# One kernel, three layers on one core: three small GpSimd operations taken off, the bulk work on the routed output put elsewhere in GpSimd's order, and a second buffer for y

## The reference, cut to what matters

```python
def layer1(x):                                   # x: (16, 512, 128)
    z = _rmsnorm(x_normed, gamma1) @ W_in.T
    gate, xc = z[..., :256], z[..., 256:]
    xc = causal_conv4(xc) + conv_b
    alpha = exp(-8 * softplus(forget_base) * sigmoid(forget)); beta = sqrt(1 - alpha**2 + 1e-6)
    h = linear_recurrence(alpha, beta * sigmoid(inp) * xc)      # a scan over tokens
    x_h = x_normed + (gelu(gate) * h) @ W_out.T
    t   = x_h + (gelu(mgate) * mx) @ W_shrink.T                  # of rmsnorm(x_h) @ W_grow.T
    x3  = x + layernorm(t)
    y   = router_weight * (layernorm(x3) @ w_expert + b_expert)  # top-1 of 8, capacity 100 of all tokens
    return x3 + layernorm(y)
```

## Time and profile before

| | us |
|---|---|
| median of 3 runs (1336.96 to 1337.99) | 1337.04 |
| the profiled execution, its own time | 1337.33 |
| its span, first to last instruction | 1335.6 |
| granted TensorE clock, mean | 0.975 |
| busy in the span: PE / DVE / ACT / POOL | 1182.7 / 1096.2 / 976.9 / 824.4 |
| layer 1's iterations 1 to 15 and the drain | from about 900 to the end |

### The profile page before, as it was taken

How to read it: one execution, slowest core, us unless ns; L and a number is a source line. 1 busy time by engine, 2 the same in 40 slices (tenths; PEclk the granted TensorE clock), 3 DMA queues, 4 the chain that set the end, 5 groups by cost and what they waited for, 6 DMA issues and landing times.

```text
span 1335.6 us, 25924 instructions
## 1 busy us (share of the span) xinstructions
PE 1182.7 (89%) x8560; PEld 481.8 (36%) x8560; DVE 1096.2 (82%) x2355; ACT 976.9 (73%) x1780; POOL 824.4 (62%) x1091
## 2 busy tenths in 40 slices
PE   1689999999999999999999998997989999999962
PEld 0223232333333333333333332333544555555542
DVE  3877999999999999999999999965676867867757
ACT  1267887787788878788778878778767778787750
POOL 6304447466466566565665655276688898998863
PEclk9889999999999999999999999899999999999986
DMA  1131011011010110110110110000000000000000
GB/s 50 52 90 43 28 44 41 30 43 40 29 44 32 37 43 33 38 45 30 41 45 27 37 35 16 2 1 1 1 0 17 8 11 15 9 16 9 9 17 24
DMA packets 52516, 37.86 MB, mean 28 GB/s; under 512 B 8864, under 2 KB 51744, under 8 KB 52384
## 3 DMA queue, kind: packets, MB, share of 16 engines
q1 hardware_dynamic: 52384, 36.22, 8.5%
HBM read 6.31 MB, written 4.19 MB: 8 GB/s over the span
## 4 chain that ended last, share of the span: by engine, by line
PE 35%; POOL 20%; DVE 20%; issue 13%; ACT 8%; SPq 4%; DMA 0%; ACTq 0%; POOLq 0%; DVEq 0%
PE bank_pair L201 10%; PE bank L182 9%; DVE neg_max L493 9%; PE bank_pair L169 4%; PE bank_pair L228 3%; SPq L644 3%; PE bank_pair L210 3%; POOL probs L1574 3%; ACT probs L381 2%; PE bank_pair L235 2%; POOL rs_y L1546 2%; DVE probs L1181 1%; DVE y_q L472 1%; PE bank_pair L800 1%; POOL x_all L1523 1%
## 5 line engine op out<-in xcount | busy, mean ns | idle before, releaser
L381 ACT ACTIVATE probs<-bank 128x512 f32<-128x512 f32 x1024 | 569.3, 598 | 165.8 <-PE bank L182 163.3
L493 DVE TENSOR_REDUCE neg_max<-bank_pair 128x2 f32<-128x1024 f32 x512 | 610.6, 1216 | 87.3 <-PE bank_pair L169 85.4
L182 PE MATMUL bank<-q_stack,k_stack 50*128 50x512 bf16 x1024 | 352.7, 388 | 30.3 <-ACT probs L381 22.6
L201 PE MATMUL bank_pair<-probs,v_pad 128*32 128x256 f32 x4096 | 332.0, 394 | 0.4 <-issue 0.4
L169 PE MATMUL bank_pair<-k_stack,q_stack 48*128 48x512 bf16 x1024 | 291.4, 395 | 35.0 <-DMA k_stack<-k_parts 17.9
L182 PEld LDWEIGHTS bank<-q_stack,k_stack 50*128 50x128 bf16 x1024 | 79.4, 93 | 273.9 <-ACT probs L381 232.6
L201 PEld LDWEIGHTS bank_pair<-probs,v_pad 128*32 128x32 f32 x4096 | 82.9, 108 | 167.6 <-issue 161.1
L800 PE MATMUL bank_pair<-probs,w_gates 128*128 128x512 f32 x256 | 116.8, 600 | 2.0 <-issue 1.7
L567 POOL TENSOR_SCALAR tiny<-mv_b 128x4 f32<-128x4 f32 x16 | 3.7, 230 | 147.4 <-DVE mv_b L52 147.4
L522 POOL TENSOR_TENSOR q_rest<-q_rest,q_parts 128x512 f32<-128x512 f32 x16 | 20.2, 1265 | 118.6 <-ACT q_rest L325 118.6
L169 PEld LDWEIGHTS bank_pair<-k_stack,q_stack 48*128 48x128 bf16 x1024 | 53.8, 94 | 60.2 <-DVE neg_max L493 38.3
(11 more groups left out here) (253 smaller groups left out, 2217.3 us busy)
## 6 DMA issues: line engine op xcount, KB each, us to landing
q_stack<-q_parts SPq DMA_DIRECT2D x384, 32.0 KB
k_stack<-k_parts SPq DMA_DIRECT2D x384, 32.0 KB
x_all<-in_z_dram SPq DMA_DIRECT2D x16, 256.0 KB, 3.0
out_dram<-x_all SPq DMA_DIRECT2D x16, 256.0 KB, 2.3
q_stack<-max_rows SPq DMA_DIRECT2D x64, 8.0 KB
w_gates<-in_w_gates_dram SPq DMA_DIRECT2D x1, 512.0 KB, 3.5
w_in<-in_w_in_dram SPq DMA_DIRECT2D x1, 256.0 KB, 2.6
w_grow<-in_w_grow_dram SPq DMA_DIRECT2D x1, 256.0 KB, 3.9
```

Source lines behind the costliest of these rows:

```text
L182: nc.tensor.matmul(st_ps[h][:, :], k_stack[par][rows, p, c * P:(c + 1) * P], q_stack[par][rows, p, :], start=True, stop=True).then_inc(s[" ...
L201: mm = nc.tensor.matmul(acc[32 * g:32 * g + 32, cols], v_pad[bpar][:, kc, 4 * a + g, :], probs[:, at + g, cols], start=(t == 0 and kc == 0 ...
L381: nc.scalar.activation(probs[:, 4 * (n % RING) + g, :], st_ps[g % 2][:, :], ACT.Exp, scale=SCALE)\
L493: nc.vector.tensor_reduce(neg_max[j // 4][:, c, j % 4, :], score_ps[c % 2][:, :, :], AX_X, ALU.max, negate=True).then_inc(s["max_read"], 1)
```

## The change

On GpSimd three 128x4 operations of an iteration go: the scaling in `norm_h` (ScalarE's squares now carry the scale, so that their sum is the mean) and the two additions of epsilon in `rsqrt`, which VectorE does instead as `var_eps`, directly behind the statistics of t and of x3. y now alternates between two buffers by the iteration's parity (the second in q_stack), and its statistics too; VectorE waits for the subtraction of two batches ago instead of the last. With that the subtraction of the mean and the 128x512 product of batch i-4 leave the place ahead of `gate_mul(i)`. They run in iteration i+1: the first, `routed_mean`, behind `x_normed`, the second, `routed_product`, behind `root_t`. `x4_late` goes from behind `x_normed` to behind `x3_sum`, `root_ahead` from ahead of `x3_sum` to behind `root_x3`. The drain gets an order of its own.

```diff
@@ names
+    y_odd = ahead[:, T:2 * T]
@@ scalar(): mean_square
-                    A(xn2[:, c * D:(c + 1) * D], zx[par][:, c * D:(c + 1) * D], ACT.Square, accum_out=h_sum[:, c:c + 1])\
+                    A(xn2[:, c * D:(c + 1) * D], zx[par][:, c * D:(c + 1) * D], ACT.Square, scale=D ** -0.5,
+                      accum_out=h_sum[:, c:c + 1])\
@@ vector()
+        def var_eps(name, b):
+            wait(dve, s[f"stat_{name}"], C * (b + 1))
+            TS(rs[name][:, 0, :], stats[name][1][:, :, 1], EPS, None, ALU.add).then_inc(s[f"rs_{name}_step"], 1)
@@ y_of
-            return (acc_y, "y_odd") if i == NB + 2 else (y, "y")
+            return (y, y_odd)[i % 2], ("y", "y_odd")[i % 2]
@@ stats_y
+                wait(dve, s["rs_y_step"], 5 * (i - 4) - 8)
@@ routed (VectorE)
-                if i > NB + 1:
+                if i > NB + 2:
                     wait(dve, s["x4_ready"], b - 1)
                 else:
-                    wait(dve, s["yc_ready"], b)
+                    wait(dve, s["yc_ready"], b - 1)
@@ stats_t, and stats_x3 likewise
+                var_eps("t", i - 3)
@@ exps_inv
-                wait(dve, s["rs_y_step"], 5 * b)
+                wait(dve, s["rs_y_step"], 5 * b - 4)
@@ pool(): rsqrt
-            TS(r[:, 0, :], mv[:, :, 1], EPS, None, ALU.add).then_inc(q, 1)
@@ norm_h
-                TS(r[:, 0, :], h_sum[:, :], 1.0 / D, None, ALU.mult).then_inc(q, 1)
-                TT(r[:, 2, :], r[:, 0, :], half_neg, ALU.pow).then_inc(q, 1)
+                TT(r[:, 2, :], h_sum[:, :], half_neg, ALU.pow).then_inc(q, 2)
@@ routed_root, routed_sum
-                if i > NB:
-                    return
-                wait_apart(gp, s["x4_ready"], b, past_wait)
-                TT(rows(acc_y), rows(y), per_token(stats["y"][1][:, :, 0]), ALU.subtract).then_inc(s["yc_ready"], 1)
+        def routed_mean(i):
+            if live(i, -4):
+                b = i - 4
+                wait_apart(gp, s["stat_y"], C * (b + 1), past_wait)
+                wait_apart(gp, s["x4_ready"], b, past_wait)
+                TT(rows(acc_y), rows((y, y_odd)[i % 2]), per_token(stats[("y", "y_odd")[i % 2]][1][:, :, 0]), ALU.subtract).then_inc(s["yc_ready"], 1)
-        def routed_sum(i):
+        def routed_weight(i):
...
                 TT(rs["y"][:, 2, :], rs["y"][:, 1, :], top[:, 7, :], ALU.mult).then_inc(s["rs_y_step"], 1)
+        def routed_product(i):
...
                 TT(rows(acc_y), rows(acc_y), per_token(rs["y"][:, 2, :]), ALU.mult).then_inc(s["yn_ready"], 1)
                 if i >= NB:
                     x4(b)
@@ order of an iteration on GpSimd
             x_normed(i)
-            x4_late(i)
+            routed_mean(i - 1)
             norm_h(i)
             root_t(i)
+            routed_product(i - 1)
+            x3_sum(i)
+            x4_late(i)
+            root_x3(i)
             root_ahead(i)
-            x3_sum(i)
-            root_x3(i)
             roots_ahead(i)
             routed_root(i)
-            routed_sum(i)
+            routed_weight(i)
             gate_mul(i)
```

More of the change, by code:

```diff
@@ L1326, in stats_x3 @@
                 aggregate("x3", "x3", i - 3)
+                var_eps("x3", i - 3)
         def gated_in(i):
@@ L1478, in rsqrt @@
         def rsqrt(name, b):
-            q, mv, r = s[f"rs_{name}_step"], stats[name][1], rs[name]
-            wait_apart(gp, s[f"stat_{name}"], C * (b + 1), past_wait)
-            TS(r[:, 0, :], mv[:, :, 1], EPS, None, ALU.add).then_inc(q, 1)
+            q, r = s[f"rs_{name}_step"], rs[name]
             wait_apart(gp, q, 2 * b + 1, past_wait)
@@ L1503, in norm_h @@
                 wait_apart(gp, s["stat_h"], C * (b + 1), past_wait)
-                TS(r[:, 0, :], h_sum[:, :], 1.0 / D, None, ALU.mult).then_inc(q, 1)
-                wait_apart(gp, q, 2 * b + 1, past_wait)
-                TT(r[:, 2, :], r[:, 0, :], half_neg, ALU.pow).then_inc(q, 1)
+                TT(r[:, 2, :], h_sum[:, :], half_neg, ALU.pow).then_inc(q, 2)
                 wait_apart(gp, q, 2 * b + 2, past_wait)
@@ L1540, in routed_root @@
                 wait_apart(gp, s["stat_y"], C * (b + 1), past_wait)
-                var = stats["y_odd" if i == NB + 2 else "y"][1][:, :, 1]
+                var = stats[("y", "y_odd")[i % 2]][1][:, :, 1]
                 TT(top[:, 5, :], top[:, 4, :], var, ALU.mult).then_inc(q, 1)
@@ L1576, in pool @@
         if drain:
+            routed_mean(NB - 1)
+            routed_product(NB - 1)
             x4_late(NB)
-            routed_root(NB)
-            routed_sum(NB)
             norm_h(NB)
             gate_mul(NB)
+            routed_root(NB)
+            routed_weight(NB)
             root_t(NB)
+            routed_mean(NB)
             x3_sum(NB)
+            routed_product(NB)
             norm_h(NB + 1)
@@ L1592, in pool @@
             routed_root(NB + 1)
-            routed_sum(NB + 1)
+            routed_weight(NB + 1)
             routed_root(NB + 2)
-            routed_sum(NB + 2)
+            routed_weight(NB + 2)
             routed_root(NB + 3)
-            routed_sum(NB + 3)
+            routed_weight(NB + 3)
         else:
             x_normed(i)
-            x4_late(i)
+            routed_mean(i - 1)
             norm_h(i)
@@ L1603, in pool @@
             root_t(i)
+            routed_product(i - 1)
+            x3_sum(i)
+            x4_late(i)
+            root_x3(i)
+            point(between, i, "x3")
             root_ahead(i)
-            x3_sum(i)
-            root_x3(i)
             roots_ahead(i)
-            point(between, i, "x3")
             routed_root(i)
-            routed_sum(i)
+            routed_weight(i)
             gate_mul(i)
```

## The result

The changed kernel takes 1328.37 us, median of 4 runs (1326.51 to 1329.51), against 1337.0 before, also of 4 runs: a ratio of 0.9935 (95% interval 0.9922 to 0.9947). It is faster, by 8.6 us, where 21.8 was forecast; 1328.4 lies above the range given. The profiled execution takes 1328.57, its span 1326.7, mean granted clock 0.977. Among the runs further down one of e1's four was a slow one, 3857.98; its median and ratio are those of the other three.

A forecast was written before the change was run, and what follows sets the result against it. GpSimd was taken as the bound, TensorE 1.3 behind with floor 22.6. Gains 1.6 + 2.4 + 12.2 + 2.1 + 2.0 + 1.8 - 0.3 = 21.8 off 1337.33 gave 1315.5; 1312 to 1318 (0.62), outer range 1311 to 1322.

The forecast's parts named there:

- What bounds the kernel: Full iterations: GpSimd is the bound at 24.39 us, TensorE follows 1.3 behind, with its own floor at 22.6.
- What is late next, gh: Ahead of `wout`: gh's halves come at 21.8 and 23.0, slack 0.8 and 0.5, so TensorE's wait goes whole.
- The small operations: GpSimd, each iteration: three 128x4 operations removed save 0.24 + 0.23 + 0.23 = 0.70 us.
- The order: GpSimd, each iteration: moved bulk work covers waits on VectorE, which fall from 1.66 to 0.6, saving 1.06 us.
- The first rival: Product holds `norm_t` up: x3 and all behind 1.0 later, iteration 23.0 to 23.6, total about 1320; chance 0.14.
- second rival: New order brings nothing, waits of 1.66 stay, only 0.70 goes: 23.7 an iteration, total 1323.5; chance 0.08.
- Iterations 5 and 6: First iterations of the gain: 1.6 us from an earlier `wout` in 5, 2.4 us in 6.
- Iteration 15 and the drain's head: 2.0 us from no clock fall and a shorter `wout`, 1.8 us from `gate_mul(16)` ahead of batch 12's bulk work.
- The drain's tail: Batch 12's work put ahead of `norm_h(17)`, which had 3.50 idle before it, gives back about 0.3 us.
- The fourth rival: The clock: a fall costs 1.6; in iterations 5, 6 or drain 1317 to 1319, one avoided 1313.6; chance 0.10.
- The third rival: Slower: GpSimd's powers hold up VectorE's taps and scans, iteration 25.2 or so, total 1345; chance 0.04.
- VectorE's `var_eps`: Two added 128x4 operations an iteration, 0.2 us each at most, costing nothing, or 0.2 if their cover is gone.

The follow-up runs named there:

- e1: The kernel before with only the three small 128x4 operations taken off GpSimd, order and drain as before; 1328.74 us, ratio 0.9947.
- e3: The changed kernel with the 128x512 product directly behind the subtraction and `root_ahead` back behind `root_t`; 1318.9 us, ratio 0.9873.
- e4: The changed kernel with the 128x512 product between `x3_sum` and `x4_late` and `root_ahead` back behind `root_t`; 1318.05 us, ratio 0.9864.
- e6: e4 with another drain order, batch 12's work filling GpSimd's idle time ahead of `norm_h(17)`; 1317.6 us, ratio 0.9856.
- e7: e4 with one more 128x512 GpSimd product, of another tensor into a spare buffer, beside `norm_t`; 1323.52 us, ratio 0.9903.
- e10: The changed kernel, own drain, with 12 and 16 unread TensorE transposes in two idle stretches of the drain; 1325.17 us, ratio 0.9912.
- e11: e6 with batch 12's subtraction, product and sum behind `norm_h(17)` and `root_x3(16)`, and unread transposes in four idle drain stretches; 1314.12 us, ratio 0.983.
- e5: The changed kernel with only its drain reordered, batch 12's work filling GpSimd's idle time ahead of `norm_h(17)`; 1328.56 us, ratio 0.9937.

## Why the prediction was wrong, point by point

- **What bounds the kernel**, and TensorE's floor of 22.6: right. e3 and e4 have it, 22.61, with `wout` at 1.95.
- **What is late next, gh**: right. In e3 and e4 TensorE doesn't wait for gh.
- **The small operations**: 0.70 forecast, 0.62 alone (e1). Near.
- **The order, the step that failed**: "behind `root_t` the product covers VectorE's `norm_t` as `root_ahead` did, and the 0.25 stays", with "I take no contention". The 0.25 became 0.93, since `norm_t` took 1.83. The row that I went by, a 128x4 power beside `norm_x3`, says nothing of a 128x512 product; nor does the nearer one that I passed over, `root_ahead`'s power beside `norm_t` itself. The waits came to 1.58 in place of 0.6: 0.68 from there, 0.27 from a wait for ScalarE that I had not counted. Work went down by 0.60 (22.73 to 22.13), not 0.70. Together 0.98 + 0.1 is the missing 1.1 an iteration.
- **The first rival** had this mechanism with a price of 1.0 and 0.35 to 0.95 left an iteration; measured are 0.7 and 1.1, since I let stalls fall away that only moved. The period, 23.7, is the second rival's, for the first one's reason. It had 0.14.
- **Iterations 5 and 6**: 4.0 forecast, 1.3 came. The stretch from `gate_mul(5)` to (6) is 25.49 after and 24.24 in e6: the same loss as in the full ones. From (4) to (5) it is 27.57 after, 25.97 in e4, but 27.55 in e6, which has e4's order there. So it differs from one execution to another, and the traces show by what: TensorE's block `gate_in` in that stretch takes 5.29 in the kernel after and 5.22 in e6, 3.60 in the kernel before and in e4. The granted clock is 0.50 from 1000 to 1002 in the kernel after. This fall, 1.7, is more than the 1.1 of miss. Before, then after:

```profile
1000.73 3.60 PE L800 MATMUL bank_pair<-probs,w_gates 128*128 128x512 f32 x8
```

```profile
998.21 5.29 PE L801 MATMUL bank_pair<-probs,w_gates 128*128 128x512 f32 x8
```

- **Iteration 15 and the drain's head**: 3.8 forecast, 3.6 measured, by TensorE's starts 1.6 of 2.0 and 2.0 of 1.8. Without the long idle time the fall of the clock in iteration 15 went (1.6); the 0.35 that `wout(15)` was to lose stayed, 2.30. With `gate_mul(16)` first, 9.55 pass from `wout(16)` to it in place of 11.51.
- **The drain's tail**, a mis-sized term: -0.3 forecast, -4.4 measured. I counted GpSimd's work ahead of `norm_h(17)`, too low, as that came 1.0 later and not 0.3, and not that TensorE, idle 2.90 there in place of 1.75, would go on with a lower clock. The fourth rival, the clock, had 1.6 for one fall and a total inside the range; in the drain it fell in two places at once, 3.1, and once more in iteration 5.
- **The third rival**, slower, was to decide "from 1.8 of added time"; with the slack of 0.5 that the same text gives gh, it is 2.3. The scans took 2.36, and nothing hangs on it.
- **VectorE's `var_eps`**, "0.2 each at most": 0.47 for the first (the row above) and up to 1.02 in other orders, beside bulk work of GpSimd. What the longer ones cost was not measured by itself.
- **Iteration 4**, "not POOL's, and I count nothing": 2.4 gained, of which 1.6 is a fall of the clock that went. Before, TensorE waited 1.87 for xn, GpSimd's product, and the next block ran at a lower clock (granted 0.50 from 972 to 974); after, it waits 1.55 and the block takes 3.60. e1 has the same 1.55 and 3.60, so the small operations are enough for it. I had not forecast it; with the fall in iteration 5, 1.7 the other way, the two cancel by luck. Before, then after:

```profile
970.89 0.80 PE L791 MATMUL bank<-ident,probs 128*128 128x128 f32 x4 [1.87 <-POOL probs L782]
971.48 5.20 PE L800 MATMUL bank_pair<-probs,w_gates 128*128 128x512 f32 x8
```

```profile
970.67 0.65 PE L792 MATMUL bank<-ident,probs 128*128 128x128 f32 x4 [1.55 <-POOL probs L783]
971.16 3.60 PE L801 MATMUL bank_pair<-probs,w_gates 128*128 128x512 f32 x8
```

The errors add up: iterations 5 to 14 18.3 forecast and 7.1 measured, 11.2 too much; iteration 15 and the head 0.2; the tail 4.1; less the 2.4 of iteration 4 and the 0.2 ahead of it: 12.9, which is 21.8 - 8.9.

## What to carry to other kernels

Before bulk work of GpSimd is put beside a VectorE operation, look in the trace for a row in which work of the same size stands beside that operation; a 128x4 neighbour told nothing of a 128x512 one. Where it must stand there, the hold-up costs nothing as long as GpSimd has more to do than the held operation takes (e7), and one place further down there may be none (e4, 1.1 less an iteration). In a drain or any thin stretch count what an added wait does to TensorE's clock, not only to the order, and look whether spare matmuls into a free bank keep it high (3.1 us for 28 transposes in e10; two further fillers in e11 brought nothing sure). A total that is near can hide falls of the clock at one place and gains at another: compare the same TensorE block in both traces before a difference is called unexplained.

## What the runs showed of the hardware

- Four 128x128 tensor_scalar of VectorE (f32, a mean and a factor per token) took 1.11 beside a 128x4 power of GpSimd that had started 0.06 before, 1.83 beside a 128x512 product that had started 0.07 before. A 128x4 one beside such work took 0.47 to 1.02, where it takes 0.17 alone.
- An idle time of 3.48 ahead of `shrink(18)` left the clock up in the kernel before (2.02) and came with a fall in e7 (3.65, the row below). Of 2.09 and 2.60 ahead of the transposes for `shrink(17)` the shorter came with a fall (e5, 3.47), the longer with none (e6, 1.95). The length of the last idle time alone doesn't decide it. In e11, with 24 transposes ahead of `xn2_t(16)`, `wout(17)` still took 3.41, little less than 3.75 without them.

```profile
1291.60 3.65 PE L810 MATMUL bank_pair<-w_shrink,probs 128*128 128x128 f32 x16 [3.48 <-DVE shifted L1218]
```
